# Values' products moved to steps 1 and 5 of the next body, router products folded into them, late chain and row transfers respaced

## The reference

```
h = batchnorm(relu(patches(x) @ W.T + b)) * gamma + beta
xn = layernorm(h)
q, k, v = xn @ Wq.T + bq, xn @ Wk.T + bk, xn @ Wv.T + bv      # 8 heads of 16
h = h + softmax(q @ k.T / 4) @ v @ Wo.T + bo
logits = layernorm(h) @ Wr + br                              # 8 experts, top 1
gate = softmax(top-1 logit over one entry)                   # from the top logit alone
h = h + gate * (relu(layernorm(h) @ W1[e] + b1[e]) @ W2[e] + b2[e])
```

## Time and profile before

| | |
|---|---|
| median of 3 timed runs | 1265.26 us |
| the profiled execution's own time | 1258.58 us |
| its span | 1256.4 us |
| mean granted TensorE clock | 0.973 of full speed |
| PE, DVE, ACT, POOL busy | 93%, 85%, 75%, 55% |

### The profile page before, as it was taken

How to read it: one execution, slowest core, us unless ns; L and a number is a source line. 1 busy time by engine, 2 the same in 40 slices (tenths; PEclk the granted TensorE clock), 3 DMA queues, 4 the chain that set the end, 5 groups by cost and what they waited for, 6 DMA issues and landing times.

```text
span 1256.4 us, 52556 instructions
## 1 busy us (share of the span) xinstructions
PE 1172.1 (93%) x21379; PEld 741.3 (59%) x21379; DVE 1063.9 (85%) x2742; ACT 941.5 (75%) x2477; POOL 690.8 (55%) x908
## 2 busy tenths in 40 slices
PE   6569999999999999999999999999999889888996
PEld 3324656555555555565655555555644459887996
DVE  7479899999999999999999999999999737665774
ACT  5427888888887878787888888887877776554664
POOL 2062437566573838474756657483823435765664
PEclk9779999999999999999999999999999999888998
DMA  8143132322313131313223232313130353224331
GB/s 192 43 82 83 51 75 69 81 83 64 92 55 93 49 101 40 107 55 94 71 81 81 66 89 58 93 49 102 41 106 26 101 144 101 80 83 131 104 105 47
DMA packets 79434, 102.61 MB, mean 82 GB/s; under 512 B 15916, under 2 KB 72995, under 8 KB 78734
## 3 DMA queue, kind: packets, MB, share of 16 engines
q1 hardware_dynamic: 70624, 79.02, 23.5%
q0 software_dynamic: 8384, 20.22, 5.2%
q10 hardware_dynamic: 186, 0.02, 0.0%
HBM read 60.76 MB, written 38.93 MB: 79 GB/s over the span
## 4 chain that ended last, share of the span: by engine, by line
PE 62%; DVE 17%; issue 7%; POOL 6%; ACT 2%; DMA 1%; POOLq 0%; SPq 0%; DVEq 0%; ACTq 0%
PE psum L1340 38%; PE psum L1405 13%; DVE half_max L1179 12%; POOL out_dram L771 4%; PE psum L1490 4%; PE psum L1504 3%; PE psum L1345 2%; ACT arena L873 2%; DVE stats L979 1%; DVE rows L1053 1%; POOL arena L408 1%; PE psum L1360 1%; DMA arena<-max_rows 1%; PE psum L1481 0%; DVE neg_max L998 0%
## 5 line engine op out<-in xcount | busy, mean ns | idle before, releaser
L1179 DVE TENSOR_REDUCE half_max<-psum 128x1 f32<-128x373 f32 x1536 | 759.9, 533 | 58.1 <-PE psum L1340 50.7
L873 ACT ACTIVATE arena<-psum 128x373 f32<-128x373 f32 (+1 forms) x1536 | 653.8, 489 | 146.0 <-PE psum L1340 133.6
L1340 PE MATMUL psum<-k_rows,arena 96*32 96x373 bf16 x6144 | 516.5, 327 | 14.2 <-DVE half_max L1179 4.9
L1340 PE MATMUL psum<-arena,k_rows 98*32 98x373 bf16 x6144 | 512.7, 324 | 9.2 <-ACT arena L873 4.8
L1405 PE MATMUL psum<-arena,values 128*32 128x373 f32 (+1 forms) x3072 | 311.9, 477 | 0.4
L1340 PEld LDWEIGHTS psum<-k_rows,arena 96*32 96x32 bf16 x6144 | 172.1, 96 | 192.1 <-DVE half_max L1179 102.9
L1340 PEld LDWEIGHTS psum<-arena,k_rows 98*32 98x32 bf16 x6144 | 175.3, 95 | 174.8 <-ACT arena L873 75.3
L628 POOL DMA_INDIRECT routed_rows_dram<-rows,pos_i x96 | 97.6, 1017 | 174.4 <-PE psum L1340 104.7
L771 POOL DMA_INDIRECT out_dram<-arena,slot_id x101 | 119.9, 1188 | 74.6 <-issue 42.4
L1405 PEld LDWEIGHTS psum<-arena,values 128*32 128x32 f32 (+1 forms) x3072 | 97.3, 110 | 20.8 <-issue 2.3
L922 ACT COPY arena<-psum 128x128 f32<-128x128 f32 x101 | 26.8, 265 | 84.0 <-PE psum L1481 52.1
(11 more groups left out here) (223 smaller groups left out, 1621.4 us busy)
## 6 DMA issues: line engine op xcount, KB each, us to landing
arena<-q_parts_dram SPq DMA_DIRECT2D x192, 93.2 KB, 2.4
k_rows<-k_parts_dram SPq DMA_DIRECT2D x192, 93.2 KB, 2.4
arena<-routed_rows_dram SPq DMA_DIRECT2D x101, 130.0 KB
q_parts_dram<-q_part SPq DMA_DIRECT2D x48, 186.5 KB
k_parts_dram<-k_part SPq DMA_DIRECT2D x48, 186.5 KB, 1.9
arena<-in_x_t_dram SPq DMA_DIRECT2D x3, 703.1 KB, 15.5
seq<-in_w_dram SPq DMA_DIRECT2D x1, 2048.0 KB, 8.6
seq<-in_w_dram SPq DMA_DIRECT2D x8, 256.0 KB, 7.6
```

The costliest lines, as they stand in the source:

```text
L873: nc.scalar.activation(probs[0:kn(kt), G % N_P, j, :], st_bank[s % N_ST][0:kn(kt), 0:HALF], ACT.Exp).then_inc(s_exp, 1)
L1179: nc.vector.tensor_reduce(half_max[:, m:m + 1], mx_bank[m % N_MX][:, 0:HALF], AX.X, ALU.max)\
L1340: last = nc.tensor.matmul(dst[n:n + m], weights[:, n:n + m], moving, start=start, stop=stop)
```

## The change

The diff does five things. The fills V move to the head of `FILLS`, at steps 1 and 5, with `STAGE` 1: body i makes the values of sequence i+1 there, out of the same `xn_t` that body i-1 filled. The router products leave HTOK; instead `wv_sb` and `wr_c` lie side by side in one tile `wv_wr`, and V multiplies both at once, with 136 moving columns in place of 128. What comes out is the product of the normalised rows, so GpSimd multiplies it back by the standard deviation (`std`, `logit_share`) and then adds `row_c`. `SCATTER_AT` moves by 0 to 2 steps. The scatters of sequence 14 move from a block before the first store to places behind stores 0, 2, 5, 7, 10 and 12 (`SCATTER14`). And the tables of the late chain are spread over more turns: merge 27, root 28, logits 29, norms 30 to 41 with gaps, `gate_diff` 38, `gate_exp` 43, `gate` 45, scatters 50 to 62 with gaps, the slot table 51 to 56, and the eight padding writes one at a time at 59 to 69. A sixth piece gives the scores five banks from step 39 where `is_body(i, LAST_BODY)` holds; `LAST_BODY` is B = 16 (L400 before), and bodies run to 15.

```diff
-    SCATTER_AT = (0, 3, 6, 9, 12, 15)
+    SCATTER_AT = (0, 4, 8, 10, 12, 16)
     EARLY_AT, EARLY_T_AT, EARLY_SLOTS_AT, WEIGHTS_AT = 50, 62, 66, (69, 72, 75)
+    SCATTER14 = (0, 2, 5, 7, 10, 12)
     LATE_TURN, LATE_INV, LATE_MULT, LATE_BACK = (0, 1), 2, 3, (4, 5)
-    LATE_PROJ, LATE_REST, LATE_LN2 = (8, 13), (10, 15), (16, 17, 18, 19, 20, 21)
-    LATE_IDS, LATE_MERGE, LATE_RSTD, LATE_LOGITS, LATE_NORM = 21, 22, 23, 24, (25, 26, 27, 28, 29, 30)
-    LATE_ROUTE, LATE_RANK, LATE_RANKS = (27, 28, 29, 30, 31, 32), 35, (36, 37, 38, 39, 40)
-    LATE_DIFF, LATE_EXP, LATE_GATE, LATE_SCATTER = 31, 34, 38, (43, 44, 45, 46, 47, 48)
-    LATE_TABLE, LATE_ROWS, LATE_SLOTS = (42, 43, 44, 45, 46, 47), 50, 52
-    PAD_AT = (50, 52, 54, 56)
+    LATE_PROJ, LATE_REST, LATE_LN2 = (8, 18), (16, 20), (21, 22, 23, 24, 25, 26)
+    LATE_IDS, LATE_MERGE, LATE_RSTD, LATE_LOGITS, LATE_NORM = 26, 27, 28, 29, (30, 32, 34, 37, 39, 41)
+    LATE_ROUTE, LATE_RANK, LATE_RANKS = (36, 37, 38, 39, 40, 41), 44, (45, 46, 47, 48, 49)
+    LATE_DIFF, LATE_EXP, LATE_GATE, LATE_SCATTER = 38, 43, 45, (50, 53, 56, 58, 60, 62)
+    LATE_TABLE, LATE_ROWS, LATE_SLOTS = (51, 52, 53, 54, 55, 56), 59, 61
+    PAD_AT = (59, 60, 62, 63, 65, 66, 68, 69)
+    WIDE_AT, WIDE_BANKS = 39, (3, 5, 0, 1, 2)
...
-        FILLS = (("HTOK", 0, 9), ("HTOK", 1, 13), ("PROJ", 0, 17), ("PROJ", 1, 27), ("MAX1", 0, 41), ("XNT", 0, 46),
-                 ("XNT", 1, 49), ("Q", 0, 53), ("Q", 1, 57), ("K", 0, 61), ("K", 1, 65), ("V", 0, 73),
-                 ("RANK", 0, 77), ("V", 1, 85), ("MAX0", 0, 88))
+        FILLS = (("V", 0, 1), ("V", 1, 5), ("HTOK", 0, 9), ("HTOK", 1, 13), ("PROJ", 0, 17), ("PROJ", 1, 27), ("MAX1", 0, 41), ("XNT", 0, 46),
+                 ("XNT", 1, 49), ("Q", 0, 53), ("Q", 1, 57), ("K", 0, 61), ("K", 1, 65), ("RANK", 0, 77),
+                 ("MAX0", 0, 88))
...
+        def st_of(i, s):
+
+            if is_body(i, LAST_BODY) and s >= WIDE_AT:
+                return psum[:, WIDE_BANKS[(s - WIDE_AT) % len(WIDE_BANKS)], :]
+            return st_bank[s % N_ST]
...
                 if s in PAD_AT:
-                    e = PAD_AT.index(s) * 2
-                    pad_regions(sp, (e, e + 1))
+                    pad_regions(sp, (PAD_AT.index(s),))
...
+            def logit_share(i, b):
+
+                pool.wait_ge(s_free, fill(i, "V", 1))
+                pool.wait_ge(s_hwr, 3 * b + 1)
+                nc.gpsimd.tensor_tensor(h_wr0[:, :, :], h_wr[:, b % 4, :, :],
+                                        std[:, :].unsqueeze(2).to_broadcast([128, NT, E]), ALU.mult).then_inc(s_hwr, 1)
+                pool.wait_ge(s_hwr, 3 * b + 2)
+                nc.gpsimd.tensor_tensor(h_wr[:, b % 4, :, :], h_wr0[:, :, :],
+                                        row_c[:, :].unsqueeze(1).to_broadcast([128, NT, E]), ALU.add).then_inc(s_hwr, 1)
...
+                if live(i, 1):
+                    logit_share(i, i + 1)
...
-                    nc.gpsimd.tensor_tensor(h_wr[:, b % 4, :, :], h_wr[:, b % 4, :, :],
-                                            row_c[:, :].unsqueeze(1).to_broadcast([128, NT, E]), ALU.add)
+                    nc.gpsimd.tensor_tensor(std[:, :], var_eps[:, :], rstd[:, :], ALU.mult).then_inc(s_hwr, 1)
...
-            scatter_ready(B - 2)
-            for t in range(NT):
-                scatter(t)
-
             def late(s):
 
                 r = B - 1
+                if s == SCATTER14[0]:
+                    scatter_ready(B - 2)
+                if s in SCATTER14:
+                    scatter(SCATTER14.index(s))
...
-                nc.scalar.copy(values[(i + 2) % 3][:, 3 * k:3 * (k + 1), :, 0:DH],
-                               bank(i, "V", k)[:, 0:3 * D].rearrange("p (t h d) -> p t h d", t=3, h=H)).then_inc(s_free, 1)
+                both = bank(i, "V", k)[:, 0:3 * (D + E)].rearrange("p (t d) -> p t d", t=3)
+                nc.scalar.copy(h_wr[:, (i + 1) % 4, 3 * k:3 * (k + 1), :], both[:, :, D:D + E])
+                nc.scalar.copy(values[(i + 1) % 3][:, 3 * k:3 * (k + 1), :, 0:DH],
+                               both[:, :, 0:D].rearrange("p t (h d) -> p t h d", h=H)).then_inc(s_free, 1)
...
                 if name == "V":
                     for n in range(3):
                         t = 3 * part + n
-                        last = quad(to[:, D * n:D * (n + 1)], xn_t[:, D * t:D * (t + 1)], wv_sb[:, :])
+                        last = quad(to[:, (D + E) * n:(D + E) * (n + 1)], xn_t[:, D * t:D * (t + 1)], wv_wr[:, :])
...
                     last = transposes(to, part, lambda t: h_t[:, D * t:D * (t + 1)])
-                    for n in range(3):
-                        t = 3 * part + n
-                        last = quad(to[:, 3 * D + E * n:3 * D + E * (n + 1)], h_t[:, D * t:D * (t + 1)], wr_c[:, :])
```

More of the change, by code:

```diff
@@ L181, in audio_tower @@
         raw = sb("raw", [128, NT, E])
+        std = sb("std", [128, NT])
+        h_wr0 = sb("h_wr0", [128, NT, E])
         scaled = sb("scaled", [128, NT, E])
@@ L808, in copy_out @@
                 in_turn(act, i, name, part)
-                if name == "HTOK":
-                    nc.scalar.copy(h_wr[:, (i + 2) % 4, 3 * part:3 * (part + 1), :].rearrange("p t e -> p (t e)"),
-                                   bank(i, name, part)[:, 3 * D:3 * D + 3 * E])
                 nc.scalar.copy(dst, bank(i, name, part)[:, 0:3 * D]).then_inc(s_free, 1)
@@ L892, in body @@
                                     q_or_k(i, name, part, k)
-                        if s == EMPTY_AT["V", part] and live(i, 2):
+                        if s == EMPTY_AT["V", part] and live(i, 1):
                             values_out(i, part)
@@ L1431, in body @@
                             pe.wait_ge(s_mrow, i * 64 + 32 * (g + 1))
[L1432 to L1433 removed]
+                        if is_body(i, LAST_BODY) and s >= WIDE_AT:
+                            pe.wait_ge(s_red, B * STEPS)
+                            pe.wait_ge(s_exp, scores(i, s) - len(WIDE_BANKS))
+                        else:
+                            wait(pe, s_exp, scores(i, s) - N_ST)
+                        quad(st_of(i, s)[0:kn(kt), 0:HALF], k_rows[par][0:KM, h, D * kt:D * kt + kn(kt)],
                              q_rows[par][0:KM, h, qh * HALF:(qh + 1) * HALF]).then_inc(s_st, 1)
```

23 lines of the change are left out of this document (12 added, 11 removed).

## The result

The changed kernel takes **1285.36 us** (median of 4 runs, 1283.04 to 1289.73), the kernel before 1264.72 us: a ratio of 1.0164, 95% interval 1.0144 to 1.0184, so 20.6 us slower. The forecast was 1243.3 us, range 1230 to 1257. It had the wrong sign.

The account below looks back on a forecast made before the run. TensorE was taken as the bound, VectorE close behind. Late chain -16.7, bodies 0 to 13 -6.3, bodies 14 and -1 +0.5 each, scatters 0 sum to -22.0 us: 1265.26 to 1243.3 us, range 1230 to 1257.

Parts of the forecast that it names:

- The bodies: Bodies 0 to 13, moved V fills and dropped router products: -0.45 us a body, -6.3 us in all.
- I take the net of TensorE and nothing for the balance, -0.41 to -0.5: Per body: TensorE's net saving counted, better balance between engines counted as nothing, -0.45 us taken.
- The removal at 73 and 85 gives most of 0.65 each.: Steps 73 and 85 lose 0.65 us each; VectorE had idled behind TensorE there, so most is gain.
- rival D: VectorE bounds steps 73 to 94, removal gives nothing, new fills count fully: +1.38 us a body, 1268.9 us; chance 0.08.
- Steps 1 and 5 get 0.69 each, part of it filled idle.: V fills at steps 1 and 5 add 0.69 us each, partly in time TensorE had waited for VectorE.
- HTOK's 0.49 gives little.: Router products leaving HTOK save TensorE 0.49 us a body, worth little since VectorE sets the pace behind step 6.
- Costed at nothing: ScalarE's copies, GpSimd's two new operations (some 0.5 us a body), SCATTER_AT one step later and the five banks: 0 us.
- The late chain: Slot turns 27 to 53: spreading GpSimd's late work removes 16.7 of 25.7 us lost, bounds 3 to 24.
- for the eight single writes of padding, the table work ... and the load of slot 72 ... I take 5 us: Part of the 25.7 us lost in turns 27 to 53 that stays: 5 us, half of the third place's 10.2.
- rival C: GpSimd becomes the bound of turns 27 to 62, its DMAs slowed by VectorE's copies: 1257.2 us; chance 0.20.
- Sequence 14's scatters: Turns 0 to 12: spreading them behind stores costs 0 us, between -2 and +2.
- The budget of time: Turns 0 to 12: 0.41 us to spare a turn leaves GpSimd 3.6 us behind, inside the 6.5 the buffers allow.

## Why the prediction was wrong

**The bodies** (-6.3 us forecast; +19.5 measured by the medians with the bodies alone, 1.3 to 1.5 us each). The failed step is "I take the net of TensorE and nothing for the balance, -0.41 to -0.5". Its parts:

- *The removal at 73 and 85 gives most of 0.65 each.* It does only with `place` out of the way. As the change stands, VectorE's gain runs into GpSimd's `k_part`, and the removal is worth nothing: the difference to the kernel before is +0.51 ahead of it, -0.15 behind step 73 and +0.48 behind step 88. The prediction read VectorE's idle time behind TensorE as room. The price of rival D, +1.38 a body, is near the measured 1.5; its mechanism was half right: VectorE does set the pace from step 85 on, but because one of its 140 instructions waits for GpSimd, which neither rival D nor the forecast had. The row that would have told it, 0.42 us for an instruction of which its equals take 0.20, was in the trace.
- *Steps 1 and 5 get 0.69 each, part of it filled idle.* They cost 0.53 and 0.55 in the changed kernel, 0.47 and 0.58 without the fold: about a fifth was filled idle.
- *HTOK's 0.49 gives little.* With V in place the fold gives 0.3 a body, so more than little. With V moved, the 0.3 won at HTOK is followed by a loss of 0.8 between steps 9 and 22 in the changed kernel, which the forecast did not have and whose cause is open. So removal, fills, HTOK and this loss make 0 + 1.1 - 0.3 + 0.8 = 1.6 us, the whole growth of the median body.
- *"Costed at nothing", GpSimd's two new operations:* its busy time rises by 0.48 us a body, as said. No row shows that somebody waits for them. `SCATTER_AT`, costed at nothing as well, was never tried alone.

**The late chain** (-16.7 forecast). That turns 27 to 53 take some 58 us was right in the run with the late part alone (58.4), the waits for `logits` and `g_diff` are gone, and of the granted clock two lower windows of 3.4 us each are left between 1115 and 1178 us. What failed is the step "for the eight single writes of padding, the table work ... and the load of slot 72 ... I take 5 us", taken inside turns 27 to 53: the scatters and pads moved past turn 53 and lost 11.3 us there, in stops of 2 to 4 us (no run separates scatters from pads), where the forecast said that a new stop of over 3 us would make it wrong. GpSimd did not become the bound as in rival C: of its 40 DMAs between the closes of turns 27 and 61 seven took over 1.3 us, the mean was 1.12, and a store began at most 3.2 us behind its turn's close.

**Sequence 14's scatters** (0 forecast, -2 to +2). They cost 5.9 us in the runs. The budget of time, 0.41 us to spare a turn, did not decide it: TensorE stops at turns 4, 8 and 13 with stops of 3.4 to 4.3 us, and nothing in the forecast priced those.

**The sum:** bodies +19.5 and late part +3.0 give +22.5 by the medians, +17.2 and +2.9 give +20.1 by the ratios, and +20.6 was measured, so the two halves account for the result. Right were the router products' saving when alone, and that the five banks come into no body. The last body was to be as long as before: from its first scores to the close of turn 0 it takes 56.93 us before, 57.74 with the new bodies alone, and 59.86 in the trace of the changed kernel, where the granted clock is at half (1.2 GHz) from 1020.3 to 1027.1 us; the other two have no such stretch there. That is probably part of why this execution lies above its kernel's median.

## What to carry to other kernels

Before an instruction is made to come earlier, look at what every engine is doing at the new time: an instruction that takes twice as long as its equals may be waiting for somebody, and may then wait for all that was won. Here one table entry moved by two steps gave 9 us in the kernel before, where the whole change lost 20.6. A DMA that GpSimd issues between turns of a pipeline should be priced by a probe in a free turn, not by its duration, or tried as a plain DMA on SyncE's queue, where the same rows cost nothing here. And two edits that each free TensorE should be run apart, since what one gains the other can lose. A difference of 0.3 us a body between two traces means little until an unchanged body of the same chip stands beside it.

## What the runs showed of the hardware

- A VectorE product of two SBUF tensors, 0.20 us alone, takes as long as GpSimd's running `k_part` product (128x746) still needs: 0.42, 0.86 and 1.03 to 1.06 us, ending within 0.1 us of it in 129 of 130 bodies of the 13 traces with `place` at 82. It is not so against every GpSimd instruction. With `place` at 84 it starts inside `g_inv` (128x6, also two SBUF inputs) and takes 0.20 us all the same, as here in the run with V moved:

```profile
622.09 0.20 DVE L1102 TENSOR_TENSOR place<-place,onehot 128x48 f32<-128x48 f32 x1
621.61 1.35 POOL L674 TENSOR_TENSOR g_inv<-g_exp,minus_one 128x6 f32<-128x6 f32 x1
```

- GpSimd's DMAs in a row, with 0.30 us between, go with completions of TensorE that come 2 to 4 us late, while TensorE and ScalarE wait for nothing that the profile names but "remote" or "issue". An extra one costs 2.3 us with rows of 1040 B and 3.8 us with 4 B a partition (one execution each); the same rows as plain writes from SyncE cost nothing.
- TensorE's clock stayed granted in full (2.4 GHz) at turns 4 and 8 of the changed kernel, although it stood still for 3 to 4 us twice; the drop to half (1.2 GHz) came at 1085 us, after the third stop.
